# A ranker's row fetches: SyncE and ScalarE share three more fields, ScalarE issues eight weight loads, three row buffers each

## What is computed

```python
x0 = emb[ids].reshape(ids.shape[0], -1)          # 2048 x 1664
x = x0
for i in range(3):
    s = x @ cross_w[i]
    x = x0 * s[:, None] + cross_b[i] + x
h = relu(x0 @ w1 + b1)                           # 1664 -> 1024
h = relu(h @ w2 + b2)                            # 1024 -> 512
h = relu(h @ w3 + b3)                            # 512 -> 256
y = sigmoid(concatenate([x, h], axis=1) @ out_w + out_b)
```

## Time and profile before

| | us |
|---|---|
| median of 3 runs | 513.7 |
| lowest and highest | 512.95, 513.92 |
| the profiled execution | 512.91 |
| its span, first to last instruction | 511.1 |

### The profile page before, as it was taken

One profiled execution on the slowest core, in us unless ns is written; L12 is line 12 of the kernel. 1 busy time (PEld: TensorE's weight loads), 2 busy tenths in 40 slices (PEclk: granted clock), 3 DMA queues, 4 the chain that ended last, 5 costly groups with the idle time before them and its releaser, 6 DMA issues.

```text
span 511.1 us, 14003 instructions
## 1 busy us (share of the span) xinstructions
PE 478.2 (94%) x2912; PEld 441.8 (86%) x2912; DVE 263.3 (52%) x610; ACT 26.3 (5%) x42; POOL 369.2 (72%) x397
## 2 busy tenths in 40 slices
PE   2599899999998999999999998999999999999997
PEld 1399798999998898989889897888989998899996
DVE  5667555545453545535454552645544554545435
ACT  4542000000000000000000000000000000000012
POOL 5777777777777777777777777777777777777730
PEclk9999999999999999999999999999999999999999
DMA  8981111111111111111111111111111111111100
GB/s 240 386 287 29 30 27 29 27 30 29 29 27 30 28 29 28 28 30 27 28 27 31 28 27 29 30 27 29 26 29 30 27 28 27 31 28 28 28 17 1
DMA packets 18270, 24.59 MB, mean 48 GB/s; under 512 B 8013, under 2 KB 9000, under 8 KB 18184
## 3 DMA queue, kind: packets, MB, share of 16 engines
q0 software_dynamic: 12480, 12.80, 13.2%
q1 hardware_dynamic: 4186, 9.71, 5.3%
q10 hardware_dynamic: 1518, 1.18, 0.7%
HBM read 24.41 MB, written 0.01 MB: 48 GB/s over the span
## 4 chain that ended last, share of the span: by engine, by line
PE 71%; POOL 12%; issue 7%; DMA 6%; DVE 2%; ACT 0%; DVEq 0%; POOLq 0%
PE l_bank L739 55%; POOL x_raw L361 12%; DMA x_raw<-in_L_rec_emb,idx 6%; PE x_bank L739 4%; PE x_bank L751 4%; PE h_bank L793 3%; PE h_bank L835 1%; PE l_bank L824 1%; DVE x_raw L505 1%; PE h_bank L763 1%; DMA ids<-in_r_ids 1%; PE h_bank L739 1%; PE l_bank L763 0%; DVE h1T_lo L534 0%; DVE h1T_hi L516 0%
## 5 line engine op out<-in xcount | busy, mean ns | idle before, releaser
L361 POOL DMA_INDIRECT x_raw<-in_L_rec_emb,idx x390 | 368.4, 945 | 121.3 <-issue 100.9
L739 PE MATMUL l_bank<-w_hi,xT_hi 128*128 128x342 f32 (+1 forms) x624 | 145.4, 333 | 0.0
L739 PE MATMUL l_bank<-w_lo,xT_hi 128*128 128x342 f32 (+1 forms) x624 | 137.7, 321 | 0.0
L739 PE MATMUL l_bank<-w_hi,xT_lo 128*128 128x342 f32 (+1 forms) x624 | 137.5, 320 | 0.0
L739 PEld LDWEIGHTS l_bank<-w_lo,xT_hi 128*128 128x128 f32 x624 | 106.6, 190 | 0.0
L739 PEld LDWEIGHTS l_bank<-w_hi,xT_lo 128*128 128x128 f32 x624 | 106.0, 189 | 0.0
L739 PEld LDWEIGHTS l_bank<-w_hi,xT_hi 128*128 128x128 f32 x624 | 103.6, 190 | 2.3
L512 DVE CAST xT_hi<-x_bank 128x256 fp32r<-128x256 f32 (+1 forms) x86 | 38.5, 448 | 96.5 <-PE x_bank L751 96.5
L505 DVE COPY_PREDICATED x_raw<-past,x_bank 128x256 f32<-128x256 int32 (+3 forms) x96 | 44.7, 466 | 41.8 <-DMA x_raw<-in_L_rec_emb,idx 40.2
L751 PE MATMUL x_bank<-identity,x_raw 128*128 128x128 f32 x208 | 39.5, 278 | 16.7 <-DVE x_raw L505 16.6
L739 PE MATMUL l_bank<-w_hi,h1T_hi 128*128 128x512 f32 x120 | 48.7, 406 | 1.0 <-DVE h1T_lo L534 1.0
(11 more groups left out here) (98 smaller groups left out, 319.5 us busy)
## 6 DMA issues: line engine op xcount, KB each, us to landing
ids<-in_L_rec_emb SPq DMA_DIRECT2D x1792, 0.2 KB
ids<-in_L_rec_emb ACTq DMA_DIRECT2D x1536, 0.2 KB
w_raw<-in_L_rec_w SPq DMA_DIRECT2D x18, 512.0 KB, 12.9
x_raw<-in_L_rec_emb,idx POOLq DMA_INDIRECT x390, 2.4
b_rows<-in_L_rec_b ACTq DMA_DIRECT2D x1, 512.0 KB, 7.3
b_rows<-in_L_rec_b ACTq DMA_DIRECT2D x1, 256.0 KB, 8.5
ids<-in_r_ids SPq DMA_DIRECT2D x1, 207.0 KB, 2.6
b_rows<-in_L_rec_b ACTq DMA_DIRECT2D x1, 128.0 KB, 9.0
```

The lines of the kernel that those rows point to most:

```text
L361: pool.indirect_dma_start(out=dst, out_offset=None, in_=emb, in_offset=rows).then_inc(landed, 16)
L739: done = pe.matmul(bank[:, 0:b - a], x[:, k, :], w[:, k, a:b], start=(k == 0 and n == 0), stop=(k == last_k and n == 2))
```

## The change

Field 24 of tile 13 is no longer POOL's: SyncE issues its rows 0 to 55, ScalarE its rows 56 to 127. In tile 15 the fields 23 and 25 are shared in halves of 64 rows; field 20, which was ScalarE's, is POOL's. The shared rows are written straight into `x_buf`, so that `place` has nothing to copy for them; instead the engine waits, before the first of them, until TensorE has transposed the group that stood there two tiles earlier, and VectorE waits for their landing in `make_whole`. SyncE and ScalarE have three row buffers each instead of four and two. SyncE issues ten weight loads and then its rows; ScalarE issues four behind its third `split_hi` and four more behind its sixth. ScalarE's first 32 rows are issued in pieces of 4, 8, 4 and 16 within `first_step`, the first as soon as the addresses are there, instead of 16 within it and 16 after it. POOL issues 389 gathers instead of 390.

```diff
-    SP_TILES = list(range(2, TILES))
+    SP_TILES = list(range(2, TILES - 1))
 ...
-    SP_BUFS = 4
-    ACT_TILES = [2, 3, 5, 6, 7, 8, 10, 11, 12, 13, 14, 15]
+    SP_BUFS = 3
+    ACT_TILES = [2, 3, 5, 6, 7, 8, 10, 11, 12, 13, 14]
     ACT_FIELD = ROWS_CHUNK * FPK
-    ACT_BUFS = 2
-    ACT_FIRST = 16
+    ACT_BUFS = 3
+    ACT_FIRST = [4, 8, 4, 16]
+    SHARED = [(TILES - 3, GROUPS[-1][-1] * FPK, 56), (TILES - 1, LAST_GROUPS[-1][-1] * FPK + 1, 64), (TILES - 1, LAST_GROUPS[-2][-1] * FPK + 1, 64)]
 ...
     def of_pool(t, f):
-        return not (t in SP_TILES and f == sp_field(t) or t in ACT_TILES and f == ACT_FIELD)
+        return not (t in SP_TILES and f == SP_FIELD or t in ACT_TILES and f == ACT_FIELD or (t, f) in [s[:2] for s in SHARED])
 ...
+    SP_LOADS = 10
+    ACT_LOADS = 14
 ...
+        def shared_free(t, f):
+
+            return seen(t - 2) + next(g for g, ks in enumerate(groups(t - 2)) if f // FPK in ks) + 1
 ...
         def _(sync):
             sync.dma_start(ids[:, QUICK:TILES * F], r_ids.rearrange("(p t) f -> p (t f)", p=P)[:, QUICK:TILES * F]).then_inc(ids_loaded, 16)
-            for n, (name, k, m) in enumerate(LOADS):
-                src = {"w1": w1, "w2": w2, "w3": w3}[name][k * P:(k + m) * P, :].rearrange("(m p) c -> p m c", m=m)
-                sync.dma_start(parts(n)[0], src).then_inc(weights_loaded[n], 16)
+            for n in range(SP_LOADS):
+                sync.dma_start(parts(n)[0], weights(n)).then_inc(weights_loaded[n], 16)
 ...
+                fetch(SP_FIELD, t, 0, P, sp_rows[i % SP_BUFS], sp_landed[i % SP_BUFS])
+                for i, (u, f, cut_at) in enumerate(SHARED):
+                    if u == t or t == SP_TILES[-1] and u > t:
+                        sync.wait_ge(x_transposed, shared_free(u, f))
+                        fetch(f, u, 0, cut_at, x_buf[u % 2][:, f * E:(f + 1) * E], shared_landed[i])
 ...
+            def load_weights(ns):
+                for n in ns:
+                    act.dma_start(parts(n)[0], weights(n)).then_inc(weights_loaded[n], 16)
+
+            def fetch_shared(i):
+                t, f, cut_at = SHARED[i]
+                act.wait_ge(x_transposed, shared_free(t, f))
+                for p in range(cut_at, P, ACT_REGS):
+                    regs = [act.alloc_register(f"act_row_shared{i}_{p + j}") for j in range(min(ACT_REGS, P - p))]
+                    row = AT_ROWS.index((f, t))
+                    act.load(regs, at_bytes[row:row + 1, p:p + len(regs)])
+                    for j, reg in enumerate(regs):
+                        at = act.snap(reg, donate=True, min_val=0, max_val=(2 * H - 1) * ROW)
+                        act.dma_start(x_buf[t % 2][p + j:p + j + 1, f * E:(f + 1) * E].bitcast(U8),
+                                      emb_bytes[:, bass.DynSlice(at, ROW)], bounds_check="skip_entire_dma").then_inc(shared_landed[i], 16)
 ...
                         split_hi(n)
                         if n == 0:
                             cross_hi()
+                        if n == 2:
+                            load_weights(range(SP_LOADS, ACT_LOADS))
+                            act.wait_ge(sp_idx_ready, 1)
+                            fetch(ACT_FIRST[0])
+                    if g == 0:
+                        load_weights(range(ACT_LOADS, len(LOADS)))
                     if g == 1:
                         load_rows()
-                    if g == len(FIRST_GROUPS) - 1:
-                        act.wait_ge(sp_idx_ready, 1)
-                        fetch(ACT_FIRST)
+                    if g > 0:
+                        fetch(ACT_FIRST[g])
                     x_hi(0, g)
-                fetch(ACT_REGS - ACT_FIRST)
-                while fetched[0] < P * len(ACT_TILES):
-                    fetch(ACT_REGS)
+                for j, t in enumerate(ACT_TILES):
+                    while fetched[0] < P * (j + 1):
+                        fetch(ACT_REGS)
+                    for i, (u, _, _) in enumerate(SHARED):
+                        if u == t or t == ACT_TILES[-1] and u > t:
+                            fetch_shared(i)
 ...
+                for i, (u, f, _) in enumerate(SHARED):
+                    if u == t and f in range(a, a + n):
+                        dve.wait_ge(shared_landed[i], 16 * P)
```

More of the change, by code:

```diff
@@ L58, in dcn_ranker_kernel @@
     SP_FIELD = ROWS_CHUNK * FPK + 1
-    SP_LAST = LAST_GROUPS[-1][-1] * FPK + 1
-    def sp_field(t):
-        return SP_LAST if t == TILES - 1 else SP_FIELD
-    SP_BUFS = 4
-    ACT_TILES = [2, 3, 5, 6, 7, 8, 10, 11, 12, 13, 14, 15]
+    SP_BUFS = 3
+    ACT_TILES = [2, 3, 5, 6, 7, 8, 10, 11, 12, 13, 14]
     ACT_FIELD = ROWS_CHUNK * FPK
-    ACT_BUFS = 2
-    ACT_FIRST = 16
+    ACT_BUFS = 3
+    ACT_FIRST = [4, 8, 4, 16]
+    SHARED = [(TILES - 3, GROUPS[-1][-1] * FPK, 56), (TILES - 1, LAST_GROUPS[-1][-1] * FPK + 1, 64), (TILES - 1, LAST_GROUPS[-2][-1] * FPK + 1, 64)]
     ACT_REGS = 32
-    ONE_RUNS = [(SP_FIELD, range(2, TILES - 1)), (SP_LAST, range(TILES - 1, TILES)), (ACT_FIELD, range(2, 4)), (ACT_FIELD, range(5, 9)), (ACT_FIELD, range(10, 16))]
+    ONE_RUNS = [(SP_FIELD, range(2, TILES - 1)), (ACT_FIELD, range(2, 4)), (ACT_FIELD, range(5, 9)), (ACT_FIELD, range(10, 15))]
+    ONE_RUNS += [(f, range(t, t + 1)) for t, f, _ in SHARED]
     AT_ROWS = [(f, t) for f, tiles in ONE_RUNS for t in tiles]
-    assert sorted(AT_ROWS) == sorted([(sp_field(t), t) for t in SP_TILES] + [(ACT_FIELD, t) for t in ACT_TILES])
+    assert sorted(AT_ROWS) == sorted([(SP_FIELD, t) for t in SP_TILES] + [(ACT_FIELD, t) for t in ACT_TILES] + [(f, t) for t, f, _ in SHARED])
     ROW = E * 4
@@ L160, in dcn_ranker_kernel @@
         clamped, wrap = b1_rows[:, 0:TILES * F], b1_rows[:, TILES * F:2 * TILES * F]
-        ONE_BY_ONE = len(SP_TILES) + len(ACT_TILES)
+        ONE_BY_ONE = len(SP_TILES) + len(ACT_TILES) + len(SHARED)
         assert (SP_BUFS + ACT_BUFS) * E + ONE_BY_ONE <= TILES * F
@@ L217, in parts, with weights @@
             return [w[:, k:k + m, 0:WIDTH // m] for w in of]
+        def weights(n):
+            name, k, m = LOADS[n]
+            return {"w1": w1, "w2": w2, "w3": w3}[name][k * P:(k + m) * P, :].rearrange("(m p) c -> p m c", m=m)
+        def shared_free(t, f):
+            return seen(t - 2) + next(g for g, ks in enumerate(groups(t - 2)) if f // FPK in ks) + 1
         def half_of(part, i):
@@ L267, in dcn_ranker_kernel @@
         act_placed = sem("act_placed")
+        shared_landed = [sem(f"shared_landed{i}") for i in range(len(SHARED))]
         xT_hi_ready = sem("xT_hi_ready")
@@ L294, in _, with fetch @@
             sync.dma_start(ids[:, QUICK:TILES * F], r_ids.rearrange("(p t) f -> p (t f)", p=P)[:, QUICK:TILES * F]).then_inc(ids_loaded, 16)
-            for n, (name, k, m) in enumerate(LOADS):
-                src = {"w1": w1, "w2": w2, "w3": w3}[name][k * P:(k + m) * P, :].rearrange("(m p) c -> p m c", m=m)
-                sync.dma_start(parts(n)[0], src).then_inc(weights_loaded[n], 16)
+            for n in range(SP_LOADS):
+                sync.dma_start(parts(n)[0], weights(n)).then_inc(weights_loaded[n], 16)
             sync.wait_ge(sp_idx_ready, 1)
+            def fetch(f, t, a, b, rows, landed):
+                for p in range(a, b, SP_REGS):
+                    regs = [sync.alloc_register(f"sp_row{f}_{t}_{p + j}") for j in range(min(SP_REGS, b - p))]
+                    row = AT_ROWS.index((f, t))
+                    sync.load(regs, at_bytes[row:row + 1, p:p + len(regs)])
+                    for j, reg in enumerate(regs):
+                        at = sync.snap(reg, donate=True, min_val=0, max_val=(2 * H - 1) * ROW)
+                        sync.dma_start(rows[p + j:p + j + 1, :].bitcast(U8), emb_bytes[:, bass.DynSlice(at, ROW)],
+                                       bounds_check="skip_entire_dma").then_inc(landed, 16)
             for i, t in enumerate(SP_TILES):
@@ L480, in place @@
             def place(t, g):
-                if t in SP_TILES and sp_field(t) // FPK in groups(t)[g]:
+                if t in SP_TILES and SP_FIELD // FPK in groups(t)[g]:
                     i = SP_TILES.index(t)
                     dve.wait_ge(sp_landed[i % SP_BUFS], 16 * P * (i // SP_BUFS + 1))
-                    dve.tensor_copy(x_buf[t % 2][:, sp_field(t) * E:(sp_field(t) + 1) * E], sp_rows[i % SP_BUFS]).then_inc(sp_placed, 1)
+                    dve.tensor_copy(x_buf[t % 2][:, SP_FIELD * E:(SP_FIELD + 1) * E], sp_rows[i % SP_BUFS]).then_inc(sp_placed, 1)
                 if t in ACT_TILES and ACT_FIELD // FPK in groups(t)[g]:
@@ L500, in make_whole @@
                                                              for f in fields(groups(u)[g])))
-                if t in SP_TILES and sp_field(t) in range(a, a + n):
+                if t in SP_TILES and SP_FIELD in range(a, a + n):
                     dve.wait_ge(sp_placed, SP_TILES.index(t) + 1)
```

## The result

| | us |
|---|---|
| before, median of 4 runs (lowest, highest) | 513.79 (512.95, 513.92) |
| after, median of 4 runs | 529.25 (528.77, 530.28) |
| ratio after/before, 95% interval | 1.0304 [1.0291, 1.0317] |
| after, the profiled execution; its span | 529.31; 527.5 |

The kernel is 15.5 us slower. 521.8 was forecast, with 524.5 as the upper end: the direction was right, and the size nearly twice what was forecast.

The account below looks back on a forecast made before the run. POOL's gathers were taken to set the pace, with SyncE's and ScalarE's row trains nearly late. 512.91 + 5.9 (wait behind ScalarE's rows) + 2.1 (clock) + 0.5 (first stage) = 521.4, set at 521.8 towards the median; range 516.5 to 524.5.

Parts of the forecast that it names:

- What bounds the kernel, and the gather less: POOL, a gather every 1.25 us, sets the pace; 389 gathers instead of 390 make later ones 1.25 us earlier.
- The first stage: Moved weight loads are hidden at the start; delay D of `x_hi(0, 3)`, which counts fully at the end, taken as +0.5 us.
- SyncE's start: With ten weight loads ahead instead of eighteen, SyncE's first row goes out at 12.1 instead of 24.67, 12.6 us sooner.
- the 4.6 us of ScalarE's first rows: All first 32 rows go out before `x_hi(0, 3)`, so ScalarE's row 33 follows at 49.6 instead of 54.22: -4.6 us.
- the third buffer's 7.2: A third row buffer removes one wait in ScalarE's train, before the rows that went out at 340.47: -7.2 us.
- Term (1) of ScalarE's total: ScalarE issues 1608 rows, 72 more, at 0.275 us each with register loads: +19.8 us on its row train.
- What waits behind it: In tile 15, `x_hi(15, 2)` behind ScalarE's last row starts at 489.3 instead of 483.11; TensorE begins that chunk 5.9 us later.
- The clock: TensorE's clock falls in its 7 us hole in tile 15, so chunks behind start slow: +2.1 us, bounds 0 and 3.4.
- (a): Rival: ScalarE's row train is quicker, 0.270 us a row, last row by 481.9; kernel faster at 512.4; chance 0.08.
- (b): Rival: TensorE's clock stays up behind the hole in tile 15, giving 519.7 us; chance 0.07.
- (c): Rival: SyncE's rows stay queued behind the weights until 22 us, losing the 12.6 us; 524.4 or 526.5; chance 0.04.
- (d): Rival: first tile late by the full 4 to 5 us, 526, chance 0.04; or partial cost, 514 to 517, 0.05.

Follow-up runs that it names:

- Three and four: The kernel before with all SyncE and ScalarE row addresses inside the table, none skipped: 764.01 us; and with all out of bounds, every row skipped: 513.07 us.
- experiment two: The changed kernel with field 24 of the last tile shared in place of field 25, which POOL fetches: 521.78 us, 1.0169 to the kernel before.

## Why the prediction was wrong

- *What bounds the kernel, and the gather less* (-1.25 us, eaten by the wait): right as a mechanism; alone it gives 1.28 us. In after itself the last gather came at 490.2 and not near 489.1, and TensorE ran dry at 484.3 and not at 483.1. The wait hid this miss.
- *The first stage* (D = 0.5, bounds -0.5 to 5): `x_hi(0, 3)` at 47.34 against 47.27, and alone no change. Right, at its cheap end. That it came out so near 0 is partly luck: with the same first stage the same conversion came between 47.1 and 48.5 us in the traces of the other runs.
- *SyncE's start, the 4.6 us of ScalarE's first rows, the third buffer's 7.2*: right, up to ScalarE's row 1544 at 471.6.
- *Term (1) of ScalarE's total, "72 more [rows], +19.8 us", at 0.275 each*: this step failed. A row's price depends on whether it is fetched, and the 64 rows at the end are field 25, all fetched. From 471.7 to 497.8 they took 26.1 us with their two register loads, where 64 x 0.275 = 17.6: 8.5 us too few. SyncE's last row, forecast for 487.9, went out at 497.2 for the same reason. The range's 0.002 us a row for this term was an error of estimate over a mixture that stays the same; it held no change of the mixture. Before's line of SyncE's rows (under Three and four) had the warning in it: a median of 73 ns beside a maximum of 318, and a mean step of 257. So had the ids' ranges.
- *What waits behind it* (`x_hi(15, 2)` right behind the last row, then TensorE): right as a mechanism, but TensorE goes on 14.4 instead of 5.9 us later; shown by moving the conversion alone.
- *The clock* (+2.1): 2.0 measured over the stretch, 2.2 against the filled hole. Right, although the hole was twice as long. The chunks that it was priced by the earlier trace rows lie where the view gives a granted clock of 1.00, but the trace's record of the clock begins only at 29.66 us. That they ran at the lower level is an inference: three of their matmuls took 1.06 us, as three did behind the hole (at 499.78), where the granted clock is 0.53.
- Rivals: (a) needed a faster train; such a one exists, with every row skipped, but the change chose the slowest rows. (b) is refuted by the clock rows, (c) by SyncE's start at 12.25, (d) by `x_hi(0, 3)`.

The sum with the measured term is 521.4 + 8.5 = 529.9, against 529.3 in the profiled execution.

## What to carry to other kernels

An average price out of a long train holds only for more of the same train. Where a DMA may be skipped, look at the shortest, the median and the longest issue and at the data that decide between them, and give a train that is nearly late the rows that are skipped. And do not put an engine's conversion, on which the matmuls wait, behind row issues in its program: that placement alone turned a late field into 6 us more.

## What the runs showed of the hardware

- A row DMA of 256 bytes, issued from registers, takes its engine 0.173 us if it is out of bounds and skipped, and 0.334 if it is fetched (SyncE, without register loads; 73 and 228 ns of it are the issue's own row). On ScalarE the issues' medians are 90 and 230 ns. Why a fetched row costs its issuer more, no run shows.
- A short idle can be followed by a fall of the clock. In after, TensorE waited 2.26 us, until 314.69, for a gather that took 2.89 us to land, and then ran at about 1.2 GHz (from 316 to 320 the granted clock is 0.59; the same stretch of before has 1.00). The window, and the chain there:

```profile
316.00:320.00 4.00, 4.00 (x18) 4.00 (x17) 0.02 (x1) 0.00 (x0) 2.89 (x4) 0.59 0.11 25
```

```profile
311.19 2.89 DMA x_raw<-in_L_rec_emb,idx
...
315.10 7.20 PE l_bank L783 x36
```

  36 matmuls took 7.20 us there, against 5.67 at full clock. Not every such wait did this: at the same place in before TensorE waited 1.77 us, until 313.44, and the granted clock stayed at 1.00; in experiment two it waited 1.87 us, until 313.95, and the clock of 314.5 to 318 is 0.51. Nothing of it reached the end: the next tile had slack against POOL (30.0 against 28.5 us a tile), and was worked through without a wait for a gather.
